# Opening of an AdaLN attention block on one core: rope sums placed behind the low part ahead, the last tiles' norm behind the ropes, one modulation row in another bank

## What is computed

```python
mod = (silu(c) @ wmod).reshape(2, 6, 1, 512)      # wmod is 512 x 3072
sa, ca, ga, sb, cb, gb = six rows of mod          # ga, gb: sign kept, magnitude at least 0.25
h = layernorm(x) * (1 + ca) + sa
q, k = rope(h @ wq), rope(h @ wk); v = h @ wv     # 32 query heads, 8 key heads, width 128
attn = softmax(q k^T / sqrt(128), causal, sliding window of 128) v
x = x + ga * (attn @ wo)
h = layernorm(x) * (1 + cb) + sb
x = x + gb * ((silu(h w1^T + b1) * (h w2^T + b2)) @ w3^T + b3)
```

## Time and profile before

| | |
|---|---|
| time, median of 3 runs | 1497.78 us (1497.16 to 1498.67) |
| profiled execution, its own time | 1497.44 us |
| its span | 1495.7 us |
| mean granted TensorE clock | 0.999 of full speed |
| TensorE busy | 1472.5 us, 98% |
| VectorE busy | 1102.9 us, 74% |
| GpSimd busy | 863.7 us, 58% |
| ScalarE busy | 826.0 us, 55% |

### The profile page before, as it was taken

The page is one execution under the profiler, slowest core; times in us unless marked ns, Lnnn a source line. Parts: engine busy times, 40 slices in busy tenths (PEclk is TensorE's granted clock), DMA queues, the critical chain, the costliest instruction groups (busy, mean ns, idle before and its releaser), DMA issues.

```text
span 1495.7 us, 27356 instructions
## 1 busy us (share of the span) xinstructions
PE 1472.5 (98%) x7589; PEld 1223.5 (82%) x7589; DVE 1102.9 (74%) x1852; ACT 826.0 (55%) x2183; POOL 863.7 (58%) x887
## 2 busy tenths in 40 slices
PE   8799999999999999999999999999999999999999
PEld 4488888888888888888888888888888888877887
DVE  6687787877787878789787778787877868783542
ACT  4455655656555656565565655565665556552331
POOL 2356565656565655669855646555664665676333
PEclk9999999999999999999999999999999999999999
DMA  9011111110201111324311020111111101153001
GB/s 330 8 37 57 36 56 30 51 38 7 84 7 56 35 56 35 127 67 123 99 37 56 7 84 7 56 35 56 35 56 35 56 28 38 60 183 127 28 29 57
DMA packets 99217, 90.20 MB, mean 60 GB/s; under 512 B 5467, under 2 KB 73315, under 8 KB 99175
## 3 DMA queue, kind: packets, MB, share of 16 engines
q1 hardware_dynamic: 98582, 88.50, 18.8%
q10 hardware_dynamic: 432, 0.66, 0.1%
q0 software_dynamic: 160, 0.52, 0.1%
HBM read 74.98 MB, written 14.69 MB: 60 GB/s over the span
## 4 chain that ended last, share of the span: by engine, by line
PE 90%; DVE 5%; ACT 2%; POOL 2%; issue 1%; DMA 0%; DVEq 0%; POOLq 0%; ACTq 0%
PE pP L276 11%; PE pP L278 11%; PE pP L277 11%; PE pOp L276 8%; PE pOp L278 8%; PE pOp L277 8%; PE pS L278 4%; PE pS L277 4%; PE pAv L276 4%; PE pS L276 4%; PE pAv L277 4%; PE pAv L278 4%; PE pTr L286 3%; PE pXx L355 1%; PE pAv L451 1%
## 5 line engine op out<-in xcount | busy, mean ns | idle before, releaser
L1257 POOL TENSOR_SCALAR_AFFINE_SELECT pm<-pT 128x512 fp32r<-128x512 f32 x480 | 393.9, 853 | 474.2 <-DVE pT L869 474.0
L276 PE MATMUL pP<-hT,wp 128*128 128x512 f32 (+1 forms) x776 | 313.1, 404 | 3.7 <-issue 2.7
L278 PE MATMUL pP<-hT,wp 128*128 128x512 f32 (+1 forms) x776 | 302.0, 389 | 0.0
L277 PE MATMUL pP<-hT,wp 128*128 128x512 f32 (+1 forms) x776 | 300.8, 388 | 0.0
L631 ACT CAST oT<-pAv 128x512 fp32r<-128x512 f32 x128 | 75.1, 586 | 280.1 <-PE pAv L278 280.1
L1270 POOL TENSOR_TENSOR rB<-rB,tab 128x512 f32<-128x512 f32 x160 | 218.0, 1374 | 15.2 <-ACT rB L654 15.2
L643 ACT ACTIVATE pr<-pS,nb 128x128 f32<-128x128 f32 x512 | 182.4, 373 | 66.0 <-DVE nb L889 66.0
L899 DVE TENSOR_TENSOR rA<-pP,tab 128x512 f32<-128x512 f32 x160 | 110.3, 689 | 129.1 <-ACT rB L654 129.1
L276 PE MATMUL pOp<-wos,oT 128*128 128x512 f32 x512 | 201.4, 393 | 3.8 <-DVE oT L864 3.6
L278 PE MATMUL pOp<-wos,oT 128*128 128x512 f32 x512 | 199.5, 390 | 0.0
L277 PE MATMUL pOp<-wos,oT 128*128 128x512 f32 x512 | 199.3, 389 | 0.0
(11 more groups left out here) (196 smaller groups left out, 3012.7 us busy)
## 6 DMA issues: line engine op xcount, KB each, us to landing
st<-in_L_attn_wq_dram SPq DMA_DIRECT2D x64, 256.0 KB, 3.6
st<-in_L_attn_wo_dram SPq DMA_DIRECT2D x64, 256.0 KB, 3.8
h_dram<-hs SPq DMA_DIRECT2D x16, 512.0 KB, 3.9
st<-in_L_attn_wk_dram SPq DMA_DIRECT2D x16, 256.0 KB, 4.2
wm<-in_L_wmod_dram SPq DMA_DIRECT2D x4, 1024.0 KB, 10.4
st<-in_L_attn_wv_dram SPq DMA_DIRECT2D x16, 256.0 KB, 2.7
xin<-in_L_attn_x_dram SPq DMA_DIRECT2D x16, 256.0 KB, 3.5
qT<-h_dram SPq DMA_DIRECT2D x2, 2048.0 KB, 10.1
```

The costliest lines, as they stand in the source:

```text
L276: nc.tensor.matmul(o, hi_l, hi_r, start=start, stop=False, skip_group_check=True)
L277: nc.tensor.matmul(o, hi_l, lo_r, start=False, stop=False, skip_group_check=True)
L278: return nc.tensor.matmul(o, lo_l, hi_r, start=False, stop=stop, skip_group_check=True)
L1257: last = nc.gpsimd.affine_select(out=pm[:, own, part], in_=pT[:, part], compare_op=op, fill=0.0, base=0, pattern=[[0, G], [sign, P]], chan ...
```

## The change

On VectorE each rope sum moves from the next job's place to its own, right behind the low part of the job ahead. The order per job was cos(i), sum(i-1), split, low(i-1); it becomes cos(i), split, low(i-1), sum(i). The statistics and the applying of the norm of tiles 6 and 7 leave the rope loop and stand behind the last low part.

On ScalarE `first_act` of tiles 4 and 5 leaves the rope loop, and stands behind the high part of job 4. `row_copy(3, 1)` comes between tiles 5 and 6, and tile 7 comes in front of unit 0 instead of inside it. On GpSimd the two `ln_rstd` stand behind the five `rope_sin`. On TensorE `mod_row(3)` comes ahead of the transpose of tile 6.

The banks of rows 3 and 4 are exchanged: row 3 now writes `pOp`, free since row 2 was copied, and row 4 writes `pAv`, free once `first_act(5)` has read it. V's turning now waits for `first_act(6)`, which reads the same bank, and not for `first_act(7)`. No instruction is added or removed.

```diff
--- before.py
+++ after.py
@@ -198,7 +198,7 @@
 
 
         ROW_BLOCK = [0, 1, 3, 4, 2, 5]
-        row_banks = [bank[0:B, :] for bank in (pTr, pAv, pOp, pAv, pOp, pXx)]
+        row_banks = [bank[0:B, :] for bank in (pTr, pAv, pOp, pOp, pAv, pXx)]
         ln_banks = [pP0[:], pP1[:], pS[:, 0:512], pS[:, 512:1024], pTr[:], pAv[:], pXx[:], pTr[:]]
 
         def l_acted(L):
@@ -440,9 +440,9 @@
                 if r >= 2:
                     pe.wait_ge(s_wm[w], 16)
                 if r == 3:
+                    pe.wait_ge(s_rowc, 3)
+                if r == 4:
                     pe.wait_ge(l_act, l_acted(5))
-                if r == 4:
-                    pe.wait_ge(s_rowc, 3)
                 if r == 5:
                     pe.wait_ge(s_modT, 2)
                 for k in range(KT):
@@ -497,8 +497,8 @@
                 project(f0, name, 0, j, j + 1, j - 1)
                 if j < 4:
                     first_transpose(2 + j)
+            mod_row(3)
             first_transpose(6)
-            mod_row(3)
 
             regs = loop_registers(pe, "pe", (PER_J, PER_U, PER_W, 1))
             for b in range(B):
@@ -509,7 +509,7 @@
                     if b == 0 and u == 0:
                         first_transpose(7)
                         mod_row(4)
-                        pe.wait_ge(l_act, l_acted(7))
+                        pe.wait_ge(l_act, l_acted(6))
                         turn_v(f, SLOT["V"])
                         pe.wait_ge(l_chunk0, 8)
                     if b == 1 and u == 0:
@@ -784,10 +784,11 @@
                     rope_hi(f0, list(SLOT)[j - 1], 0, j - 1, j)
                 if j < 3:
                     split_weight(f0, wp[:, 0, j + 3, :], j + 3, (j + 3) % 5)
-                if j in (3, 4):
-                    first_act(1 + j)
+            first_act(4)
+            first_act(5)
+            row_copy(3, 1)
             first_act(6)
-            row_copy(3, 1)
+            first_act(7)
 
             regs = loop_registers(act, "act", (PER_J, PER_U, PER_W, PER_V, 32, 1, 16))
             for b in range(B):
@@ -798,7 +799,6 @@
                     if b == 0 and u == 1:
                         act.wait_ge(s_row, 5)
                     if b == 0 and u == 0:
-                        first_act(7)
                         v_hi(f, 0, 1)
                     jobs_act(f, u, b)
                 for u in range(2):
@@ -1122,18 +1122,14 @@
             dve.wait_ge(s_tab[0], 32)
             for i in range(5):
                 rope_cos(f0, 0, i)
-                if i:
-                    rope_sum(f0, i - 1, i)
-                if i in (3, 4):
-                    ln_apply(3 + i)
                 if i < 3:
                     split_first(3 + i)
                 if i:
                     rope_lo(f0, names[i - 1], 0, i - 1, i)
-                if i in (2, 3):
-                    ln_stats(4 + i)
-            rope_sum(f0, 4, 5)
+                rope_sum(f0, i, i + 1)
             rope_lo(f0, "Q3", 0, 4, 5)
+            ln_stats(6), ln_stats(7)
+            ln_apply(6), ln_apply(7)
             first_tile(4)
             first_tile(5)
             dve.wait_ge(s_tab[1], 32)
@@ -1345,8 +1341,8 @@
             ln_rstd(5)
             for j in range(5):
                 rope_sin(f0, 0, j)
-                if j in (2, 3):
-                    ln_rstd(4 + j)
+            ln_rstd(6)
+            ln_rstd(7)
             pool.wait_ge(s_tab[1], 32)
 
             def clear_all():
```

## The result

The changed kernel takes 1489.91 us (median of 5, 1489.4 to 1491.26) beside 1498.28 for the kernel before on the same chip. The ratio is 0.9948, 95% interval 0.9937 to 0.9959: faster by 0.52%. A second set of five executions gave 1489.64 and 0.9947 (0.9934 to 0.9961). The forecast was 1490.0, with a range of 1488.4 to 1493.2, against the median of 1497.78 then known. The spans of the profiled executions are 1495.7 and 1488.9 us, 6.8 apart.

A forecast was written before the change was run, and what follows sets the result against it. TensorE, 99% busy behind the anchor, was taken as the bound, with VectorE's opening work setting the anchor. VectorE's terms summed to 52.43 against 60.24, 7.8 us earlier: profiled 1497.44 to 1489.6, median 1497.78 to 1490.0, range 1488.4 to 1493.2.

The forecast's parts named there:

- The anchor: TensorE's start of projections for the second 512 tokens: moves from 60.24 to 52.43 us, the end by the same 7.8.
- The rival in which the gain is swallowed behind the anchor: Some later wait absorbs the gain: full loss 1497.8 us (no change 0.04), half 1494 (part loss or short clock fall 0.07).
- The ropes: Opening on VectorE and GpSimd: last low part starts at 42.24 us instead of 48.15, V's projection 1.60 us earlier.
- Who goes first: VectorE's sum against GpSimd's sine product: first to start wins, loser pays about 1.2 us; sum 0 loses, sums 1 to 3 win.
- the first rival: GpSimd's sine products win the close races at jobs 1 to 3: gain of 5.8 us, 1492.0; chance 0.19.
- The second rival: Sum 0 also wins against its sine product: last low part about 0.7 us earlier, 1489.3 us; chance 0.07.
- The norm behind the ropes: VectorE, statistics of tiles 6 and 7: 2.0 us out of the loop; second apply at 45.83, unhidden, the move's price.
- Tile 7's activation: ScalarE does it from 48.0 to 49.5 us, hidden behind VectorE, whose 1.92 us wait for it is left out.
- The bank exchange: Rows 3 and 4 swap banks: costs nothing; without it row 3 would wait for tile 5's activation at 45.3 us.
- The clock: TensorE stays at full clock despite a gap of about 1.5 us before tile 6's transpose, saving row 3's 1.69 us.
- The last rival: Clock falls in the gap before tile 6: 1494 at worst if short (0.07 with part loss), 1503 if long (slower 0.03).
- The first three cases: One or no race lost behind job 0 (1489.3 to 1491.2) 0.60, sum 0 winning too 0.07, all lost (1491.2 to 1493) 0.19.

The follow-up runs named there:

- sums and bank: Kernel before with rope sums in their new place and row 3 in the free bank ahead of tile 6's transpose: 1491.37 us, ratio 0.9959.
- row 3 ahead of V: Changed kernel with row 3 between Q3's and V's projections, V's ScalarE copy behind activations 4 and 5: 1490.08 us (one run), again 1490.37, ratio 0.9952.
- the old banks: Changed kernel with the old banks of rows 3 and 4 and row 3 behind tile 6's transpose again: 1494.38 us, ratio 0.9979.
- bank only: Kernel before with only row 3 in the free bank and ahead of tile 6's transpose: 1493.87 us, ratio 0.9977.
- norm behind only: Kernel before with only the norm of tiles 6 and 7 and the activations of tiles 4 and 5 behind the ropes: 1500.92 us, ratio 1.0019.

## Why the prediction was right

**The anchor carries the end.** Right. From the anchor to the end of the span it is 1435.5 us before and 1435.9 after. Over all traces it ranges from 1435.0 to 1437.2, a scatter of 2.2 us beside the 2 us of the opening's start. The rival in which the gain is swallowed behind the anchor is out.

**The ropes.** Right to 0.13 us. From the first cos, the last low part was to start at 42.24 - 27.10 = 15.14, and it does at 15.01 (41.89 - 26.88). V's projection was to start at 10.42 and does at 10.41. The sine product of job 4 takes 1.48 us and not about 1.8, since sum 3 starts 0.37 us ahead of it and holds it up for less.

**Who goes first.** Sum 0 lost and sums 1 to 3 won, as taken. The rule behind it, that the earlier record wins, holds in the opening of every trace from 0.03 us on, in both directions (0.28 behind loses). Sums 1 and 2 started 0.03 or 0.04 us ahead of their product sixteen times over all traces, and the sum won each time, so the first rival, in which they lose, is out. The rule does not hold for 0.02. With sums and bank the product's record starts 0.02 us ahead of sum 0's, as in the changed kernel (28.55 and 28.57), and there the sum wins. So job 0 is open at that distance; the sum won in two of eleven traces that have it in that place. The second rival, a sum 0 that wins, was real. With row 3 ahead of V the last low part comes 0.4 us earlier (14.57 against 14.97) and not 0.7, and the anchor follows by 0.4 (24.88 against 25.27). There cos 4 waits 0.54 us for Q3's swap, behind a projection that TensorE, busy all along, does no sooner. With sums and bank it gives 1.1.

**The norm behind the ropes.** The price was right: the second apply was to start 18.73 us behind the first cos and does at 18.61. But I wrote that the statistics leave the loop for 2.0 us of gain there and called the rest the price of the move; I did not separate the two. Alone the move loses 3.0 us. In the changed kernel it is worth some 0.8 us at the full clock by the working above: the ropes end 4.1 us sooner (19.12 to 15.00). From the last low part to the anchor the changed kernel takes 10.30 us. With sums and bank it is 8.87 us, of which 1.92 are the wait for tile 7; so the norm's work behind the ropes takes 3.35 us back.

**Tile 7's activation.** The prediction read the wait of 1.92 us and had tile 7 done from 48.0 to 49.5, hidden behind VectorE; it was done from 48.03 to 49.54. This part stood in the sum only as a wait left out, and it is worth more than the norm's move.

**The bank exchange.** Here the prediction said too little. It counted the exchange as costing nothing and wrote that without it row 3 would wait for `first_act(5)` at 45.3. With the old banks row 3 stood behind tile 6's transpose, which waited 4.80 us for its norm; the exchange is worth 4.3 to 5.1 us of the change.

**The clock.** This is the step that failed in the profiled execution: "I cost no low clock and save the 1.69 us". The clock fell behind the 1.28 us gap, row 4 took 1.13 us longer, and TensorE, which should have been ready 0.3 us ahead of VectorE, set the anchor 0.8 us later. In the second trace the step held, and the anchor came at 25.30 us against a forecast of 52.43 - 27.10 = 25.33. The last rival was thus half right. The clock can fall behind that gap, and on TensorE it costs what its short form said: 1.13 us of row 4 and 0.46 of the transposes against the 1.7 forecast, of which 0.8 reach the anchor. It lasted some 3.4 us, far from the 13 that would make the kernel slower. That rival's 1503 is a slip: its own terms, an anchor 0.4 us later than before and 5.7 us more behind it, give 1503.9.

**The range.** Its ends don't follow from the stated terms. The first three cases run from 1489.3 to 1493, and 0.7 us on both sides gives 1488.6 to 1493.7, not 1488.4 to 1493.2. The measured time lies inside either.

The times then agree: 7.0 and 7.8 us at the anchor in the two traces, and 8.4 and 7.7 between the medians of the two sets (1498.28 and 1497.32 before). That the forecast of the time came out to 0.1 us is in part luck: the executions of the changed kernel alone spread over 2.2 us (1489.09 to 1491.26), and the profiled one, forecast at 1489.6, took 1490.65.

## What to carry to other kernels

Moving work off a chain can lose time when another engine's queue stands behind the moved work: the norm's move cost 3.0 us with row 3 behind tile 6's transpose, and with row 3 in front of it gained about 0.8, as worked out. So read a change of several parts by running each part alone and all but one, and count the parts first: the exchange gave 3.3 us alone and nothing on top of the sums, and a fourth part, a single activation ahead of a softmax, got no run of its own and stands for some 1.9 us. Where VectorE's two-operand work meets GpSimd's, keep the order clear by more than a few hundredths of a microsecond, and insert nothing between them that turns it: 1.0 us of statistics in a wait of 0.6 us cost 1.4 us at V.

## What the runs showed of the hardware

- The same gap of TensorE is followed by 1.2 GHz in one execution and not in another: 1.28 against 1.30 us in the changed kernel, 1.83 against 1.86 us in bank only and before. The low clock came behind gaps of 1.13 us (bank only) and 1.32 us (sums and bank) too, and did not behind 1.36, 1.41 and 1.42 us in three other kernels.
- The clock did not fall in these short gaps but behind them, while TensorE was fully busy: 1.7 us behind the gap's end (45.10 and about 46.8) in the changed kernel, 1.4 us (39.11 and about 40.5) in bank only. Before, it fell 0.3 us behind the end of the 4.71 us gap (47.27 and about 47.5). In two long gaps it fell while TensorE was idle: 2.7 us into the 4.80 us gap with the old banks (40.06 and about 42.7) and 2.8 us into the 7.69 us gap of norm behind only (40.91 and about 43.7). These are single traces.
- Two records that start 0.02 us apart (GpSimd first) don't tell which of the two goes first: the sum took 1.81 or 1.82 us in five executions and 0.68 in two. At 0.03 us and more the earlier record went first in the opening of every trace.
